# Making the result weights of four tiles one slot earlier in a fused mixer and expert kernel

## The reference, cut to what matters

```
logits  = xn @ gate;  w, e = top_2(logits);  w = softmax(w)
y       = (silu(xn @ w0[e]) * (xn @ w1[e])) @ wo[e]      # for each of the two experts
x       = x + layernorm(sum over the two of w * y)
```

## Time and profile before

| | |
|---|---|
| median of 3 runs | 299.33 us (299.3 to 300.03) |
| profiled execution: span from first to last instruction | 297.5 us |
| around the span, against the median | 1.8 us |
| busy: PE, PEld, DVE, ACT, POOL | 86%, 79%, 70%, 59%, 55% |
| slots of the tiles | from 53.6 us to 282.8 us |

### The profile page before, as it was taken

One profiled execution on the slowest core, in us unless ns is written; L12 is line 12 of the kernel. 1 busy time (PEld: TensorE's weight loads), 2 busy tenths in 40 slices (PEclk: granted clock), 3 DMA queues, 4 the chain that ended last, 5 costly groups with the idle time before them and its releaser, 6 DMA issues.

```text
span 297.5 us, 8014 instructions
## 1 busy us (share of the span) xinstructions
PE 254.9 (86%) x2056; PEld 235.2 (79%) x2056; DVE 209.0 (70%) x939; ACT 176.1 (59%) x439; POOL 164.7 (55%) x187
## 2 busy tenths in 40 slices
PE   0667696899988899999999999999999999999900
PEld 0226353799987899899979998999999999999900
DVE  3786989786884587658766956787664444798875
ACT  3634358475665676766674565656566566567681
POOL 8000377784188747874776577577533333247840
PEclk9965559599999999999999999999999999999985
DMA  5899711312310132112212211333333114802047
GB/s 144 181 384 316 209 56 48 81 55 67 74 37 30 52 79 62 45 55 76 64 36 75 75 46 47 98 104 90 92 77 90 43 55 134 334 20 81 19 141 212
DMA packets 28139, 29.65 MB, mean 100 GB/s; under 512 B 4570, under 2 KB 21180, under 8 KB 28096
## 3 DMA queue, kind: packets, MB, share of 16 engines
q1 hardware_dynamic: 22832, 20.04, 23.7%
q0 software_dynamic: 4544, 8.97, 9.4%
q10 hardware_dynamic: 720, 0.13, 0.3%
HBM read 17.53 MB, written 12.05 MB: 99 GB/s over the span
## 4 chain that ended last, share of the span: by engine, by line
PE 54%; DVE 16%; POOL 10%; issue 8%; ACT 7%; DVEq 2%; DMA 1%; ACTq 1%; POOLq 0%
PE bank L1593 28%; PE bank L1630 14%; POOL expert_rows L433 5%; PE bank L1528 3%; PE bank L1544 3%; PE bank L1537 2%; DVE sb_w_now L1236 2%; PE bank L1588 2%; POOL pair_rows L446 2%; POOL sb_rs L414 1%; DVE sb_early L824 1%; DVEq L1230 1%; DMA sb_x<-in_L_attn_x 1%; ACT sb_row L546 1%; ACT sb_early L518 1%
## 5 line engine op out<-in xcount | busy, mean ns | idle before, releaser
L1593 PE MATMUL bank<-sb_xeT,sb_w_now 128*128 128x128 f32 x1136 | 140.9, 277 | 1.9 <-DVE sb_gated L1217 1.9
L1593 PEld LDWEIGHTS bank<-sb_xeT,sb_w_now 128*128 128x128 f32 x1136 | 134.6, 194 | 3.6 <-issue 3.6
L446 POOL DMA_INDIRECT pair_rows<-sb_y_rows,sb_y_pair x71 | 71.3, 1004 | 55.4 <-ACT sb_y_rows L618 38.2
L433 POOL DMA_INDIRECT expert_rows<-sb_row,sb_place x64 | 65.0, 1016 | 47.9 <-DVE sb_place L931 29.0
L1217 DVE TENSOR_TENSOR sb_gated<-bank,sb_silu 128x512 f32<-128x512 f32 x71 | 49.0, 689 | 50.9 <-PE bank L1593 35.7
L1630 PE MATMUL bank<-sb_w_raw,sb_gated 128*128 x568 | 76.2, 277 | 2.2 <-ACT sb_y_rows L618 1.4
L1630 PEld LDWEIGHTS bank<-sb_w_raw,sb_gated 128*128 128x128 f32 x568 | 69.0, 192 | 3.8 <-issue 3.6
L589 ACT ACTIVATE sb_silu<-bank 128x512 f32<-128x512 f32 x71 | 42.5, 598 | 18.0 <-PE bank L1593 15.7
L584 ACT ACTIVATE sb_xeT<-bank 128x128 f32<-128x128 f32 x71 | 19.6, 277 | 56.1 <-PE bank L1588 56.0
L607 ACT ACTIVATE sb_w_now<-sb_w_raw 128x512 f32 x71 | 44.4, 625 | 0.4 <-issue 0.4
L1236 DVE COPY sb_w_now<-sb_w_raw 128x512 f32 x71 | 32.3, 455 | 1.5 <-issue 1.5
(11 more groups left out here) (179 smaller groups left out, 276.3 us busy)
## 6 DMA issues: line engine op xcount, KB each, us to landing
sb_taken_rows<-expert_rows SPq DMA_DIRECT2D x71, 65.5 KB, 1.9
sb_w_raw<-in_L_ffn_w SPq DMA_DIRECT2D x2, 2048.0 KB, 14.7
sb_pairs_early<-pair_rows SPq DMA_DIRECT2D x3, 1024.0 KB, 7.2
out_dram<-sb_x SPq DMA_DIRECT2D x3, 512.0 KB, 3.8
pair_rows<-sb_y_rows,sb_y_pair POOLq DMA_INDIRECT x71, 2.3
sb_x<-in_L_attn_x SPq DMA_DIRECT2D x4, 256.0 KB, 5.9
expert_rows<-sb_row,sb_place POOLq DMA_INDIRECT x64, 2.5
expert_rows<-sb_pad_row SPq DMA_DIRECT2D x8, 65.5 KB
```

What stands on the lines that cost most here:

```text
L433: pool.indirect_dma_start(expert_rows[:, :], bass.IndirectOffsetOnAxis(ap=place[b % ROWS][:, k, j:j + 1], axis=0), row[b % ROWS][:, j, :], ...
L446: pool.indirect_dma_start(pair_rows[:, :], bass.IndirectOffsetOnAxis(ap=y_pair[group % 2][:, t % PAIRS:t % PAIRS + 1], axis=0), y_rows[slo ...
L1593: last = pe.matmul(to[:, n * P:(n + 1) * P], w[:, n * P:(n + 1) * P], x, start=True, stop=True)
```

## The change

Tanh and weights of a group are made in the slot of its third tile, 4g+2, instead of its fourth, 4g+3. Both ScalarE and VectorE now wait for the fourth tile's rows to have landed, which before was implied by the work on that tile. SyncE waits for `y_weight` where it waited for `y_pair`, and also until the tile that had the ring place is turned and copied (`xeT`).

```diff
-                    wait(sp, c["y_pair"], (t - RING) // PAIRS + 1)
+                    wait(sp, c["y_weight"], (t - RING) // PAIRS + 1)
+                    wait(sp, c["xeT"], t - RING + 1)
                     load_tile(t)
...
             def tanh_of_gaps(t):
-                if not is_tile(t) or (t % PAIRS != PAIRS - 1 and t != TILES - 1):
+                last = t + 1
+                if not is_tile(last) or (last % PAIRS != PAIRS - 1 and last != TILES - 1):
                     return
-                first, group = t - t % PAIRS, t // PAIRS
-                n, ring = t + 1 - first, first % RING
+                first, group = last - last % PAIRS, last // PAIRS
+                n, ring = last + 1 - first, first % RING
+                act.wait_ge(s_rows_in[last % RING], 16 * (last // RING + 1))
...
             def pairs_of_tiles(t):
-                if not is_tile(t) or (t % PAIRS != PAIRS - 1 and t != TILES - 1):
+                last = t + 1
+                if not is_tile(last) or (last % PAIRS != PAIRS - 1 and last != TILES - 1):
                     return
-                first, group = t - t % PAIRS, t // PAIRS
-                n, ring = t + 1 - first, first % RING
-
+                first, group = last - last % PAIRS, last // PAIRS
+                n, ring = last + 1 - first, first % RING
+                dve.wait_ge(s_rows_in[last % RING], 16 * (last // RING + 1))
                 for old in range(first - 2 * PAIRS, first - PAIRS):
                     wait(dve, s_y_sent[old % Y_SLOTS], 16 * (old // Y_SLOTS + 1))
                 dve.tensor_tensor(not_first[:, 0:n], taken_rows[:, ring:ring + n, D + 1],
-                                  tile_expert[:, first:t + 1],
+                                  tile_expert[:, first:last + 1],
                                   ALU.not_equal).then_inc(c["not_first"], 1)
```

## The result

The changed kernel runs in 296.78 us (median of 4 runs, 296.49 to 297.26) against 299.31 us of the kernel before (4 runs on the same chip, 298.93 to 300.03): ratio 0.9917, 95% interval 0.9896 to 0.9939. That is 2.5 us less; the forecast was 3.2 less, 296.1. The profiled execution after has a span of 295.5 us, before 297.5. One run of the experiment "Both mends" took 520.32 us and is left out of its median; no other run is far from the rest of its kernel.

What follows compares the result with a forecast made beforehand. TensorE, busy 86%, was taken to bound the kernel, so only its holes could be gained: 3.80 - 0.40 - 0.16 = 3.24 us, 299.33 to 296.1 us. Forecast 295.0 to 297.3 (chance 0.64), outer range 294.9 to 298.6.

Steps and rivals of the forecast that it cites:

- Weights ready a slot earlier: ScalarE's wait for weights goes; TensorE's holes close at the product by wo (1.76 us) and batch-row turns (2.04): 3.80 us.
- The product by wo at 1.06 without idle time: Sign in TensorE's profile after, at slots 12, 36, 44 and 68: 1.06 instead of 1.15 us, 0.36 us for four restarts.
- The turn at slot 12 keeps about 0.2, the others almost none: Sign on TensorE at s = 4: holes before turning the batch's rows close, leaving about 0.2 us at slot 12.
- The choice at s = 6: VectorE's choice of experts comes 0.54 us later behind the weights, 0.39 of it covered: cost 0.4 us, bounds 0 and 0.75.
- Statistics and places at their old time: VectorE at s = 7: 0.54 us later by the slot before, 0.54 earlier by weights leaving this slot, so unchanged.
- Slot 42: VectorE has no slack there, so the weights delay `gated` of tile 42 and open a TensorE hole: 0.16 us, bounds 0 and 0.54.
- Added waits: ScalarE's, VectorE's and SyncE's new waits for rows, old sends, weights and `xeT` cost nothing; 0.5 us a round if sends are late.
- A rule that speaks against it: At s = 2 the moved two-input VectorE instructions could slow GpSimd's chain through shared SBUF interfaces: 0.36 us, left out of the sum.
- Slower: Rival: weights delay mixed rows at s = 2 and choice at s = 6, not regained at s = 3 and 7: 300.9 us; chance 0.07.
- No difference: Rival: GpSimd's chain sets `gated` at s = 3, so TensorE's closed holes reappear there: 298.6 us; chance 0.12.
- another wait takes the place: Rival, partly closed: the norm is bound by something else or `gated` comes later, restarts give nothing: 297.3 to 298.1 us; chance 0.17.
- the change doesn't do what it says: Rival: late fourth-tile rows or old sends keep the weights from coming earlier; time as before or above; no separate chance given.

Runs made afterwards that it cites:

- Both mends: The changed kernel with VectorE's weights behind the second half of the slot and TensorE's register load ahead of the batch work: 295.05 us, ratio 0.9867 against the kernel before.
- the even groups alone: The change for groups of even number only (weights made at s = 2, used at s = 4), odd groups as in the kernel before: 294.71 us, ratio 0.9852.
- the experiment on the kernel before: The kernel before with TensorE's register load ahead of the ranks' wait and, at s = 7, mean and variance ahead of the weights: 297.14 us, ratio 0.9928.
- the odd groups alone: The change for groups of odd number only (weights made at s = 6, used at s = 0), even groups as in the kernel before: 300.33 us, ratio 1.0039.
- the change with the load first: The changed kernel with TensorE's register load for the product by wo placed ahead of the ranks' wait: 294.65 us, ratio 0.9842 against the kernel before.

## Why the prediction was right, and where it was not

The direction and most of the size were right: 296.78 against 296.1, because a gain that I had made too small and a cost that I had made much too small partly offset each other. That the total came within 0.7 us is in good part luck: the gain at s = 4 was 1.61 larger and the cost at s = 7 2.39 larger than priced, and 0.56 that slots 9 and 10 gave back is in no term of the sum.

*Weights ready a slot earlier: 3.80 forecast.* The mechanism is right and shown by the even groups alone. The size was too small. Slots 4, 12, 20, 28 and 36 became shorter by 0.47, 0.94, 0.63, 0.97 and 1.65, 4.66 in sum; the steps made it 0.36, 0.83, 0.53, 0.53 and 0.80, 3.05. I had added up only the idle times printed in the rows. At slot 28 of the kernel before the product by wo started 2.06 after the product by w1, and 1.79 after, with no idle time printed in either. TensorE before:

```profile
150.22 1.95 PE L1593 MATMUL bank<-sb_xeT,sb_w_now 128*128 128x128 f32 x16
152.28 1.15 PE L1630 MATMUL bank<-sb_w_raw,sb_gated 128*128 x8
```

TensorE after:

```profile
149.47 1.95 PE L1597 MATMUL bank<-sb_xeT,sb_w_now 128*128 128x128 f32 x16
151.26 1.06 PE L1634 MATMUL bank<-sb_w_raw,sb_gated 128*128 x8
```

0.27 of wait and 0.09 of restart lay there unseen: 0.53 + 0.27 + 0.09 make 0.89 of the 0.97. At slot 36, 0.60 of the 1.65 are costs of earlier slots given back (with the even groups alone it gains 1.05).

*The product by wo at 1.06 without idle time.* Half right: none waits for a result any more, but none takes 1.06 either. It is 1.15 at slots 12 (the row at 96.73), 36 (the row at 177.07) and 68, and 1.12 at slot 44, so the 0.36 for four restarts was not seen in them. Slot 44 became 0.12 shorter, where the terms of the sum make 0.34 + 0.09 - 0.16 = 0.27. Slot 68 had its 0.23 closed and became only 0.09 shorter: VectorE's late `gated` spread its product by w1 over 2.24 instead of 1.95.

*The turn at slot 12 keeps about 0.2, the others almost none.* Right: 0.18 at 98.06, none elsewhere.

*The choice at s = 6: 0.4 forecast, bounds 0 and 0.75.* This is the step that failed. Slots 7, 15, 23, 31 and 39 grew by 0.61, 0.31, 0.35, 0.30 and 1.22, 2.79 in sum. The choice itself came 0.55 later within slot 7, about 0.3 in slots 15, 23 and 31, and 1.23 in slot 39 (counted from the turn of the slot's tile). I had read the 0.39 between the end of the choice and the first rank product as cover. It was none: the first use of the choice was hidden, but the load queued behind the same wait was already at its limit of 0.92, as the 0.24 before the product by wo showed in the kernel before, put down to "issue". I had not followed the queue past the waiting instruction. The new wait of the first rank product for the choice, forecast as 0.1 to 0.2 in three rounds, is in none of the three; it stands in slot 39 alone, with 0.49. And "in the first round and that of 190 us the cover is longer" failed most: these are the two slots that grew most. What I had right is that some of it is swallowed by the waits for `gated`, and more than one round's. Of the three waits for `gated` that the prediction had at slots 8, 11 and 35 and said would stay (in TensorE's slots 9, 12 and 36), the first shrank from 0.80 to 0.23 (the row at 84.95), the second stayed with 0.76, and the third, 0.36, is gone. Slots 7 to 10 together are 13.19 before and 13.14 after. Net, by the even groups alone against the whole change, the odd groups' move costs 2.07 us by the medians.

*Statistics and places at their old time.* Wrong in two rounds, to the good. Counted from the turn of the tile of slot 23, mean and variance start 4.10 us later before (134.24 to 138.34) and 3.42 after (133.14 to 136.56); at slot 31 it is 3.75 and 3.43, at slots 7 and 15 within 0.1 the same. "Since GpSimd starts from them" was the right reason to look; the experiment on the kernel before shows a gain of 2.1 us when that start comes earlier together with the load.

*Slot 42: 0.16.* Right in place and size: the hole at 201.85 is 0.18 and was not there.

*Added waits: nothing, 0.5 if a send is late.* SyncE's: right, shown alone. The wait for the rows: right, no row shows it. The wait for old sends: wrong in one round, 0.64 in slot 38, a little above the bound of 0.5 that I had named; such a wait in front of the weights was also among the signs of being wrong. "In the trace no such wait shows" was no evidence, since the wait now came a slot sooner.

*A rule that speaks against it.* I had left 0.36 us out. The moved instructions lie beside a send of GpSimd at 118 us, VectorE after:

```profile
118.90 0.16 DVE L1252 TENSOR_TENSOR sb_not_first<-sb_taken_rows,sb_tile_expert 128x4 f32<-128x4 f32 x1
```

GpSimd after:

```profile
118.30 0.97 POOL L434 DMA_INDIRECT expert_rows<-sb_row,sb_place  x1 [0.30 <-issue]
119.29 0.21 POOL L412 TENSOR_TENSOR sb_sd<-sb_mv,sb_eps 128x4 f32<-128x4 f32 x1
```

The send takes 0.97, as the one without the scan beside it. The Trainium skill, page "GPSIMD Engine Reference", section "Key points", says that GpSimd contends with VectorE for shared SBUF interfaces when VectorE's instruction has two SBUF inputs, as this one has; with 4 elements nothing of it is to be seen here, nor at the send of 198.54, which has all four instructions of the weights beside it and takes 0.97 as well.

*The rivals.* "Slower" had the right place, VectorE dense from s = 6 on, and for the odd groups alone it came true (300.33). "No difference" described GpSimd's chain rightly as what sets the rounds, and was wrong in that the change leaves it as long as it is. Of "another wait takes the place" only the part on the restarts came true; of the turns' holes 0.18 is left. Of "the change doesn't do what it says" one place came true, the 0.64 in slot 38.

## What to carry to other kernels

When a producer is moved later, don't stop at the first instruction that waits for it: ask what stands behind that wait in the same queue, above all a register load, whose time shows only as a small "issue" hole. Price a move in each place where it lands: here half of the groups carried the whole gain and the other half cost 2 us. And before closing a hole on the busiest engine, follow the round's other chain to its start: the same mend was worth nothing (ratio 0.9998) with the chain as it was and 2.1 us on top of the change; together with an earlier start of the chain it gave 2.1 us too, and the share of each there wasn't measured.

## What the runs showed of the hardware

A load into TensorE's register that stands behind a semaphore wait set the next product 0.92 to 1.03 us behind the end of what was waited for, in all 15 rounds of three kernels. In the other four kernels of this study with the load there it was 0.92 to 1.10, in all 20 rounds. Ahead of the wait the product followed at 0.28 to 0.30 where the choice came late (five rounds of the change with the load first), right behind the matmuls that use what was waited for. What the 0.92 is made of wasn't separated. Four dependent instructions of 128x4 elements on VectorE take 0.54 us from the start of the first to the start of what follows (95.68 to 96.22), a good deal for 4 columns. A wait between two groups of matmuls can lie wholly in the distance of their starts (2.06 against 1.79) with no idle time printed.
